# Softmax sums kept as sixteen rows per head, and inverted whole on VectorE

## What is computed

```
attn = einsum('bhnd,bhsd->bhns', q, k) * SCALE
attn = softmax(attn, axis=-1)
o = einsum('bhns,bhsd->bhnd', attn, v)
out = o.reshape(B, N, D) @ w_o          # then the gate and the residual
```

## Time and profile before

| | |
|---|---|
| median of 3 runs | 2890.01 us (2890.00 to 2892.32) |
| span of the profiled execution | 2890.6 us |
| busy, whole span | PE 2763.0 us (96%), DVE 1732.1 us (60%), ACT 1547.7 us (54%), POOL 687.5 us (24%) |
| layers 1 to 3 | from about 655 us to the end |
| one iteration of the loop | 44.50 us in layers 1 and 2, 44.38 us in layer 3 (distance of successive oT_a multiplications) |

### The profile page before, as it was taken

How to read it: one execution, slowest core, us unless ns; L and a number is a source line. 1 busy time by engine, 2 the same in 40 slices (tenths; PEclk the granted TensorE clock), 3 DMA queues, 4 the chain that set the end, 5 groups by cost and what they waited for, 6 DMA issues and landing times.

```text
span 2890.6 us, 61852 instructions
## 1 busy us (share of the span) xinstructions
PE 2763.0 (96%) x23508; PEld 2283.7 (79%) x23508; DVE 1732.1 (60%) x3584; ACT 1547.7 (54%) x2703; POOL 687.5 (24%) x759
## 2 busy tenths in 40 slices
PE   7999999995899999999999999999999999999998
PEld 6999999993677777777777777777777777777776
DVE  2444444434676776766767667667676666666642
ACT  3444444432456565665656655656566556565653
POOL 3433343321112212222121222221211111112111
PEclk8999999996799999999999999999999999999999
DMA  5122222104435445344463443444545445444431
GB/s 161 45 80 78 70 69 69 40 8 133 94 81 114 99 102 121 90 110 119 108 143 90 104 114 92 117 103 101 134 97 139 109 88 111 95 98 108 91 81 39
DMA packets 276950, 277.90 MB, mean 96 GB/s; under 512 B 90352, under 2 KB 206432, under 8 KB 276656
## 3 DMA queue, kind: packets, MB, share of 16 engines
q1 hardware_dynamic: 264752, 251.26, 36.5%
q10 hardware_dynamic: 11904, 22.68, 2.5%
HBM read 99.03 MB, written 29.56 MB: 44 GB/s over the span
## 4 chain that ended last, share of the span: by engine, by line
PE 65%; DVE 6%; issue 2%; ACT 2%; DMA 1%; SPq 0%; POOL 0%; POOLq 0%; DVEq 0%; ACTq 0%
PE gbank L3180 12%; PE obank L3025 10%; PE gbank L3025 7%; PE obank L3032 6%; PE score L3090 4%; PE obank L3110 4%; DVE m_a L2474 4%; PE obank L3156 3%; PE score L3076 3%; PE score L3139 2%; DVE x_a L2436 2%; PE gbank L3125 2%; PE obank L3125 2%; PE gbank L3016 2%; PE gbank L3040 2%
## 5 line engine op out<-in xcount | busy, mean ns | idle before, releaser
L1968 ACT ACTIVATE p_f<-score 128x1024 f32<-128x1024 f32 (+1 forms) x576 | 567.4, 1021 | 308.7 <-PE score L3090 280.6
L2474 DVE TENSOR_REDUCE m_a<-score 128x4 f32<-128x1024 f32 x384 | 459.9, 1219 | 153.8 <-PE score L3076 153.5
L3180 PE MATMUL gbank<-w,h_c 128*128 128x256 f32 x1536 | 385.1, 390 | 1.9 <-ACT h_c L1985 1.9
L3180 PEld LDWEIGHTS gbank<-w,h_c 128*128 128x128 f32 x1536 | 277.5, 190 | 44.4 <-ACT h_c L1985 2.3
L1150 PE MATMUL m_ps<-m_comb,m_w 128*128 128x256 f32 x2304 | 295.4, 284 | 1.5 <-PEq L254 1.5
L1150 PEld LDWEIGHTS m_ps<-m_comb,m_w 128*128 128x128 f32 x2304 | 279.9, 188 | 5.0 <-issue 3.6
L2484 DVE TENSOR_REDUCE m_b<-gbank 128x4 f32<-128x308 f32 x192 | 92.2, 480 | 264.7 <-PE gbank L3125 241.2
L823 ACT ACTIVATE m_hf<-m_ps,tab 128x256 f32<-128x256 f32 x192 | 80.7, 471 | 246.8 <-PE m_ps L1150 246.8
L1845 POOL TENSOR_TENSOR o_gated<-w_o,gate_a 128x512 f32<-128x512 f32 x48 | 62.4, 1300 | 593.6 <-PE obank L3032 593.6
L765 POOL TENSOR_TENSOR m_hhl<-m_hf,m_hhl 128x512 fp32r<-128x512 f32 x96 | 125.4, 1306 | 318.6 <-DVE m_hhl L989 318.6
L3110 PE MATMUL obank<-p_f,v_s 128*20 128x256 f32 x3072 | 198.0, 387 | 0.5 <-ACT p_f L1968 0.4
(11 more groups left out here) (283 smaller groups left out, 5450.8 us busy)
## 6 DMA issues: line engine op xcount, KB each, us to landing
q_cat<-q_hl SPq DMA_DIRECT2D x288, 128.0 KB, 3.6
k_cat<-k_hl SPq DMA_DIRECT2D x288, 128.0 KB, 3.9
qc_cat<-qc_hl SPq DMA_DIRECT2D x288, 128.0 KB, 3.2
split_L<-m_cut SPq DMA_DIRECT2D x24, 512.0 KB, 5.7
x_a<-x_after_L SPq DMA_DIRECT2D x48, 256.0 KB, 2.7
x_b<-x_after_L SPq DMA_DIRECT2D x48, 256.0 KB, 4.3
kc_cat<-kc_hl SPq DMA_DIRECT2D x288, 39.0 KB, 1.9
x_after_L<-y_c SPq DMA_DIRECT2D x32, 256.0 KB, 2.4
```

The source lines that it names most:

```text
L1968: e.activation(p_f[i % 4][0:n, :], score[i % 2].ap[0:n, :, :].rearrange("p h n -> p (h n)"), ACT.Exp, scale=SCALE).then_inc(ex.sem, 1)
L2474: e.tensor_reduce(m_a[:, :, i::NPAIR].rearrange("p t h -> p h t"), score[i % 2].ap[:, :, :].rearrange("p h (t k) -> p h t k", t=TT), AX.X, ...
L3180: mm = e.matmul(B_DOWN.ap[:, tt, :], h_c[:, k, tt * P:(tt + 1) * P], weights_of(d)["w2"][:, k, :], start=(k == 0), stop=(k == MC - 1))
```

## The change

`VW` becomes 32. Values and ones alternate: column 2d of a head is value d and column 2d+1 is all ones. A group of 32 partitions then holds 16 rows of products and, between them, 16 equal rows of sums. `sums_out` copies the odd rows of both tiles to `den_a` (128x512, two DMAs of 64 rows), `pack` moves the even rows of the second tile into the odd rows of the first (one DMA), `recips` inverts `den_a` in place in two halves of 128x256, and `heads_normed` multiplies `den_a` by `u_a`, both in SBUF. The high and low parts, `rcat`, `sel`, `recips_out` and `recips_spread` go. The rows of the output projections are permuted on input to suit. The kernel is also built with a smaller scratch area for DMA descriptors (1024).

```
-VW = 20
+VW = 2 * HD
...
-            def sums_out(u, sums, buf, evac, rc, signal):
+            def sums_out(u, den, buf, evac, signal):
...
                 e.wait_ge(*evac.at(u))
-                if u:
-                    e.wait_ge(*rc.at(u - 1))
-                e.dma_start(sums[:, :], buf[16::32, :, :, :].rearrange("g t c n -> g (t c n)")
-                            ).then_inc(signal.sem, 16)
+                for i in range(TT):
+                    e.dma_start(den[i::2, :, :], buf[1::2, i, :, :]).then_inc(signal.sem, 16)
...
                 e.wait_ge(*sums.at(u))
-                for g in range(4):
-                    e.dma_start(buf[32 * g + HD:32 * g + 2 * HD, 0, :, :],
-                                buf[32 * g:32 * g + HD, 1, :, :]).then_inc(signal.sem, 16)
-
-            def recips_out(u, dst, src, rh, rl, rb, signal):
...
+                e.dma_start(buf[1::2, 0, :, :], buf[0::2, 1, :, :]).then_inc(signal.sem, 16)
...
-            def recips(u, sums, rc, r, summed, sent, rc_done, rh, rl):
-
+            def recips(u, den, c, summed, rc_done):
                 e.wait_ge(*summed.at(u))
-                e.reciprocal(rc[:, :], sums[:, :]).then_inc(rc_done.sem, 1)
+                e.reciprocal(den[:, c, :], den[:, c, :]).then_inc(rc_done.sem, 1)
+
+            def heads_normed(u, oT, den, buf, rc_done, packed, users, done):
                 e.wait_ge(*rc_done.at(u))
-                if u:
-                    e.wait_ge(*sent.at(u - 1))
-                e.tensor_copy(r[:, 0, :], rc[:, :]).then_inc(rh.sem, 1)
-                e.wait_ge(*rh.at(u))
-                e.tensor_tensor(r[:, 1, :], rc[:, :], r[:, 0, :].bitcast(F32), ALU.subtract).then_inc(rl.sem, 1)
-
-            def heads_normed(u, oT, bank, buf, rb, packed, users, done):
-                e.wait_ge(*rb.at(u))
                 e.wait_ge(*packed.at(u))
                 if u:
                     e.wait_ge(*users.at(u - 1))
-                e.tensor_tensor(oT[:, :, :], bank.ap[:, :, :], buf[:, 0, :, :], ALU.mult).then_inc(done.sem, 1)
+                e.tensor_tensor(oT[:, :, :], den[:, :, :], buf[:, 0, :, :], ALU.mult).then_inc(done.sem, 1)
...
-                e.tensor_tensor(v_s[:, :, :, 0:HD], B_V.ap[:, :, :].rearrange("p t (h d) -> p t h d", d=HD),
+                e.tensor_tensor(v_s[:, :, :, 0::2], B_V.ap[:, :, :].rearrange("p t (h d) -> p t h d", d=HD),
...
-            def recips_spread(u, bank, at, sent, on, done):
-
-                e.wait_ge(*sent.at(u))
-                if u == 0:
-                    e.wait_ge(s_sel, 6)
-                turn(bank, on, u)
-                for i in range(CC):
-                    mm = e.matmul(bank.ap[:, i, :], sel[at:at + 32, i, :], rcat[at:at + 32, :], start=True, stop=True)
-                mm.then_inc(done.sem, 1)
```

More of the change, by code:

```diff
@@ L1804, in _ @@
             e.memset(kc_cat[:, :, :].bitcast(F32), -1.0).then_inc(s_ones, 1)
-            picked = p_f[0][0:64, 0:2 * P].rearrange("s (c b d) -> s c b d", c=CC, b=8)
-            e.memset(p_f[0][0:64, 0:2 * P], 0.0).then_inc(s_sel, 1)
-            for h in range(4):
-                e.wait_ge(s_sel, h + 1)
-                e.affine_select(out=picked, in_=picked, compare_op=ALU.not_equal, fill=1.0, base=-16 * h,
-                                pattern=[[-1, CC], [-2, 8], [0, HD]], channel_multiplier=1).then_inc(s_sel, 1)
             def mlp_rstd(c):
@@ L2689, in _ @@
             self_max(1, 3)
-            self_recips(0)
+            self_recips(0, 0)
+            self_recips(0, 1)
             self_max(1, 4)
@@ L2728, in _ @@
             self_x_high(3)
-            self_recips(1)
+            self_recips(1, 0)
+            self_recips(1, 1)
             self_x_low(3)
@@ L2733, in _ @@
             self_max(2, 7)
-            cross_recips(0)
+            cross_recips(0, 0)
+            cross_recips(0, 1)
             self_sum(1)
@@ L2767, in _ @@
             values_out(3)
-            self_recips(2)
+            self_recips(2, 0)
+            self_recips(2, 1)
             self_max(3, 2)
@@ L2774, in _ @@
             self_max(3, 6)
-            cross_recips(1)
+            cross_recips(1, 0)
+            cross_recips(1, 1)
             cross_keys_low(2)
@@ L2811, in _ @@
             values_out(4)
-            self_recips(3)
+            self_recips(3, 0)
+            self_recips(3, 1)
             self_max(4, 2)
@@ L2818, in _ @@
             self_max(4, 6)
-            cross_recips(2)
+            cross_recips(2, 0)
+            cross_recips(2, 1)
             cross_keys_low(3)
@@ L2901, in _ @@
             self_normed(47)
-            self_recips(45)
+            self_recips(45, 0)
+            self_recips(45, 1)
             self_max(46, 4)
@@ L2907, in _ @@
             self_max(46, 7)
-            cross_recips(44)
+            cross_recips(44, 0)
+            cross_recips(44, 1)
             cross_keys_low(45)
@@ L2937, in _ @@
             values_out(47)
-            self_recips(46)
+            self_recips(46, 0)
+            self_recips(46, 1)
             self_max(47, 2)
@@ L2968, in _ @@
             mlp_x_low(45)
-            self_recips(47)
+            self_recips(47, 0)
+            self_recips(47, 1)
             self_heads_normed(47)
-            cross_recips(46)
+            cross_recips(46, 0)
+            cross_recips(46, 1)
             self_sum(47)
@@ L2992, in _ @@
             mlp_x_low(46)
-            cross_recips(47)
+            cross_recips(47, 0)
+            cross_recips(47, 1)
             cross_heads_normed(47)
```

135 lines of the change are left out of this document (42 added, 93 removed).

## The result

The changed kernel takes **3026.73 us** (median of 4 runs, 3020.59 to 3034.05) against 2890.65 for the kernel before: a ratio of 1.0473, 95% interval 1.0458 to 1.0488. It is 136 us slower. The forecast of 3015 was right in sign and range, and 12 us short. The profiled execution spans 3032.2 us, 141.6 more than before's 2890.6.

The account below looks back on a forecast made before the run. PE, busy 389.5 of 400 us, was taken to bound the kernel. Loop iterations (72 and 14) and units outside (5) added 91 us to 2890.6, giving 2982; clock falls added 36, about 3015 us, range 2960 to 3090.

Parts of the forecast that it names:

- iteration, layers 1 and 2: Loop iteration in layers 1 and 2: waits of +2.7, less 0.4 for the spread, plus 0.2 for loads, +2.5 us.
- iteration, layer 3: Loop iteration in layer 3, which has no xn_b: PE 1.5 us late in all, +1.2 us after gains and loads.
- The reciprocal: DVE's 128x256 reciprocal: 1.7 us by the slope between 2 and 32 columns, 3.3 us for a pair.
- The first place: PE's `self_plain` 4 waits for `self_max` 2, which stands behind the self-attention's reciprocal pair on DVE: +1.1 us.
- The second place: Behind the cross-attention's reciprocal pair: PE waits 1.5 us at `self_max_rows` and 0.5 at `cross_turned`; +2.7 us with the carried-in lateness.
- PE's own gain: Each unit's two spreading pairs go from PE, 0.43 us each, 0.86 together, less 0.2 for wider value loads.
- The written-out units: 7 units outside the loop cost some 0.7 us each, 5 us together.
- The clock: Granted clock falls behind the second place in half of 29 iterations, 2.5 us each, +36 us; none in layer 3.
- The sums' landing: Self-attention sums' DMAs land at 1565.7 to 1567.3, taken as no delay; the late end would add 0.7 us.
- Hidden reciprocals: Rival: reciprocals at 0.56 us, hidden in DVE's idle time, add no PE wait; 2858 us, chance 0.07.
- Wide loads: Rival: loads of 32 columns eat PE's gain, 34 us on the forecast; shares a chance of 0.22 with two others.
- DVE and POOL: Rival: second pair's reciprocals wait for POOL's o_gated, up to 1.3 us an iteration, 3070 us; shares 0.22 with two others.

Follow-up runs that it names:

- e1: The changed kernel with each of a side's two reciprocals inverting only the first 32 of its 256 columns, the rest left uninverted: 2854.31 us, ratio 0.9866.
- e9: The changed kernel's layout, but only four of a head's 16 equal rows of sums copied and inverted (128x128), then spread by DMA, each row 4 times: 2883.43 us.
- e2: The kernel before with 32 columns of values per head in place of 20 and the smaller DMA scratch area of 1024: 2901.98 us, ratio 1.0032.
- e3: The changed kernel with second reciprocal halves moved: self-attention's behind the next maximum, cross-attention's just ahead of its multiplication; all work kept: 2890.69 us, ratio 0.9994.
- e7: e3 with more reciprocals of the written-out units 0, 1 and 44 to 46 moved too, mostly to just ahead of their multiplication: 2895.63 us, ratio 1.0013.
- e4: The changed kernel with only the self-attention's second reciprocal half moved behind the next maximum: 2945.45 us, ratio 1.0182.
- e5: The changed kernel with only the cross-attention's second reciprocal half moved to just ahead of its multiplication: 2961.73 us, ratio 1.0241.
- e6: The changed kernel with six useless matmuls ahead of `self_plain` 4 in each loop iteration, where PE would wait: 3005.23 us, ratio 1.0390.

## Why the prediction was right, and what in it was off

| step | predicted | measured |
|---|---|---|
| reciprocal of 128x256 | 1.7 us | 1.72 us |
| waits of PE, layers 1 and 2 | 1.1 + 1.5 + 0.5 = 3.1 us | 1.19 + 1.91 = 3.1 us (against e1) |
| spreading matmuls, less loads | -0.66 us | -0.94 us (e1) |
| iteration, layers 1 and 2 | +2.5 us | +2.17 us undisturbed |
| iteration, layer 3 | +1.2 us | +1.09 us |
| written-out parts, span | +5 us | +30 us (with their clock) |
| clock, in the loop | +36 us | about +28 us |
| late sums, in the loop | 0 | about +8 us |
| waits for qc_cat's DMA, the rest | 0 | about +2 us |

The span's 141.6 us divide so: the 28 distances of the loop in layers 1 and 2 (unit 3 to 31) grew from 1251.4 to 1336.0 us, 84.6, of which 28 x 2.17 = 61 is the undisturbed part and 24 the rest; the 12 of layer 3 from 532.7 to 559.5, 26.8, of which 13 and 14; up to unit 3 858.6 became 874.3, +15.7; from unit 43 on 247.9 became 262.4, +14.5.

**The reciprocal.** The line through 2 and 32 columns held: 154, 343, 944 (e9) and 1720 ns at 2, 32, 128 and 256 columns, 6.3 and then 6.1 ns a column. The Trainium skill, "VectorE: DVE Perf Modes", section "First, the fixed hardware budget", gives the reciprocal a repeat count of 8; the estimate of 8.3 ns a column made from it isn't borne out.

**The first place** was right to 0.1 us in what PE loses (1.19 us against e1, for 1.1), and in its cause; the wait that the trace shows is 0.91. **The second place** was right in size, 1.9 against 2.0, but it split otherwise. The step missed that vc_s stands between the pair and `self_max` 7 and that one of PE's `up` products (L2988, into obank) needs the bank that it reads: PE waits some 0.5 to 0.6 us there (14.3 us in 27 iterations), and so later only 0.30 and 0.33.

**PE's own gain** was mis-sized: -0.94 and not -0.66. The loads cost 0.05 and not 0.2 (e2), and what went is then worth 0.99 and not 0.86. I had priced the cross-attention's pair like the other, at 0.43 us; from `cross_turned` to the projection of oT_b the kernel before takes 6.23 us and e1 5.63, so it held PE up by 0.60. That is nearly the whole difference between 2.5 and 2.17.

**The written-out units** were the term that failed: 7 at 0.7 us each, where they cost some 30. I counted them as loop iterations with slack, without looking at their rows or at their clock. The head from layer 1 to unit 3's oT_a and the tail from unit 43's, of before (two rows) and of after:

```profile
654.80:858.60 203.80, 161.02 (x1255) 117.46 (x1256) 121.09 (x241) 87.67 (x139) 34.63 (x50) 0.80 0.41 104
2642.70:2890.60 247.90, 229.98 (x1835) 181.43 (x1834) 122.83 (x246) 127.39 (x216) 41.22 (x43) 0.97 0.33 76
654.10:874.30 220.20, 169.55 (x1247) 123.00 (x1248) 136.12 (x232) 88.01 (x139) 32.29 (x45) 0.75 0.39 103
2769.80:3032.20 262.40, 238.69 (x1816) 187.84 (x1815) 147.42 (x236) 128.06 (x216) 41.19 (x43) 0.92 0.29 79
```

The granted clock was 0.80 and 0.97 there before, and is 0.75 and 0.92 after: with fewer matmuls PE is busy for 17 us longer (8.5 and 8.7), and it is idle for 14 us more. So, by PE's busy time, over half of this term goes with the lower clock; no run took it away by itself. The idle time is of the kinds seen in the loop: from 724 to 875 us PE waits 3.7 us at L3029 on maxima behind the reciprocals, where before has no such wait, 2.2 on xn_b (0.2 before) and 1.6 on vc_s. e3 and e7 show it from the other side: the rearrangement wins in the loop and little here, and e3's clock in these two stretches is 0.77 and 0.93.

**The clock** came near the forecast's size by a reason that was partly wrong. I had put the fall behind the second place, and none in layer 3. It falls behind the first, after a single wait of 0.91 us, where PE's stream was otherwise full (e4, e5 and e6), and it does so in layer 3 too, in five of its 12 iterations. At the second place PE waits longer in all, but in four pieces of 0.3 to 0.6 us. The two slices of rows 9 were waits of another kind, and the half that I took from them was a guess that happened to fit. After's 40 iterations take 43 us more than undisturbed ones would and before's 5, which is the 38 of the table's last three rows. By the trace of after, iteration by iteration: 11 have a fall and nothing late, 17.2 us; 5 have a fall and late sums, 14.5 us, of which DVE's wait for the sums is 3.7; 4 have late sums alone, at a clock of 1.00, 4.2 us; 2 wait for qc_cat's DMA, 6.8 us, and before has two of these as well, 5.4 us. That makes about 28 us for the clock, 16 falls at some 1.75 us, where I had 14.5 falls at 2.5; and about 8 for the late sums, which stood at nothing. That the total of 38 comes near my 36 is luck.

**The sums' landing** I had costed at no delay. It is right for 36 of the 48 units; in the other twelve DVE waited 10.5 us in all for the self-attention's sums, and three times, 14.0 us, for the cross-attention's (before: 1.7 and 5.9 us, two times each). In the loop that is the 8 us above.

**The rivals.** Hidden reciprocals would have asked for 1.15 us each, and they take 1.72; e1 shows that the 2858 of that case was right for what it supposed. Wide loads: ruled out by e2. DVE and POOL: the second pair does run beside POOL, 67 of the 96 reciprocals of den_b by the trace, and none was stretched (1691 to 1753 ns over the 96, the mean 1718 ns for the 67 and 1722 for the others).

## What to carry to other kernels

When work moves from the bounding engine to an idle one, look not at its idle share but at what stands behind the new work in its list and who waits for that: here the same instructions cost 172 us or 36 by where they stood. A short wait can cost more than itself: closing one of 0.9 us with useless matmuls won 21 us. Data that will be spread to many rows can be treated on fewer of them first, and a DMA can do the spreading if its source has enough rows (e9, 143 us under after, though only 7 under e3). Price the written-out ends of a pipelined loop by their own rows and their own clock, since their slack is not the loop's.

## What the runs showed of the hardware that I had not expected

- A wait of 0.91 us in a full PE stream can be followed by a fall of the granted clock (1.00, then 0.77 and 0.80 over 8 us), and the same wait one iteration on isn't (1.00, 1.00); what decides between the two stays open. Useless matmuls in the gap made the kernel 21 us faster.
- Loads of 32 columns take 110 ns and of 20 columns 100, and 96 of them an iteration cost 0.05 us in all.
- Two DMAs of 128 KB that read 4 rows of SBUF 16 times each kept 0.23 of the DMA engines busy and had landed 7.1 us after the first one's issue began; reading 16 rows 4 times, the share was 0.73 and one landed 2.4 us after its issue began.
- 67 reciprocals of 128x256 that ran beside POOL instructions took as long (1718 ns) as 29 that didn't (1722).
